# A decoder kernel on one core: half an expert group, a round's values, a batch's weights and two output rows change place

## What is computed

```python
x = x + _L0_attn_ref(_layernorm(x), w_qkv, w_out)          # 16 heads of 8, windows of 64, causal
x = x + _L0_xattn_ref(_layernorm(x), ctx, ctx, times, ...) # 16 heads of 8, keys and values by one of 8 buckets
x = x + _L0_ffn_ref(_layernorm(x), ...)
```

```python
y1 = _ln(x + _mha(x, in_proj_w, ...), ln1_g, ln1_b)   # 4 heads of 32; each group of 8 attends within itself
y2 = _ln(y1 + _moe(y1, wg, w1, b1, w2, b2), ln2_g, ln2_b)

# _moe: 2048 rows, 8 experts, at most 256 rows to each
gates = softmax(xf @ wg); idx = argmax(gates)
keep  = (place of the row within its expert) < 256
h = disp @ w1 + b1                    # no function between the two products
y = h @ w2 + b2
out = where(keep, gate * y, 0)
```

## Time and profile before

| | |
|---|---|
| runs | 343.11, 337.6, 341.99 us; median 341.99 |
| profiled execution | 339.86 us, span 338.1 us |
| TensorE's granted clock, mean | 0.98 |
| busy | PE 317.0 us (94%), DVE 261.2 (77%), ACT 164.7 (49%), POOL 126.8 (38%) |
| transfers | 31.89 MB, mean 94 GB/s |

### The profile page before, as it was taken

The page is one execution under the profiler, slowest core; times in us unless marked ns, Lnnn a source line. Parts: engine busy times, 40 slices in busy tenths (PEclk is TensorE's granted clock), DMA queues, the critical chain, the costliest instruction groups (busy, mean ns, idle before and its releaser), DMA issues.

```text
span 338.1 us, 12320 instructions
## 1 busy us (share of the span) xinstructions
PE 317.0 (94%) x4772; PEld 217.5 (64%) x4772; DVE 261.2 (77%) x663; ACT 164.7 (49%) x454; POOL 126.8 (38%) x208
## 2 busy tenths in 40 slices
PE   7869999999999999999999999989989999998993
PEld 3435556666666565655656556557567769887992
DVE  6874688866666899989899999856456548869996
ACT  2223546666666455463565646554424438633330
POOL 1074556100000345546224344233700006614896
PEclk9976999999999999999999999999999999999998
DMA  4962230636466174589393000000000000125212
GB/s 118 314 180 84 86 121 28 178 116 161 149 154 156 59 183 124 146 196 249 117 214 103 3 2 2 4 5 0 2 2 4 4 0 2 50 80 189 95 33 63
DMA packets 38698, 31.89 MB, mean 94 GB/s; under 512 B 4969, under 2 KB 36209, under 8 KB 38513
## 3 DMA queue, kind: packets, MB, share of 16 engines
q1 hardware_dynamic: 36064, 27.37, 28.9%
q0 software_dynamic: 1280, 3.15, 3.5%
q10 hardware_dynamic: 1296, 0.59, 0.7%
HBM read 23.40 MB, written 7.70 MB: 92 GB/s over the span
## 4 chain that ended last, share of the span: by engine, by line
PE 78%; DVE 10%; issue 5%; POOL 5%; ACT 1%; POOLq 0%; DVEq 0%
PE ps L1262 10%; PE ps L1299 10%; PE ps L1316 10%; PE ps L1272 4%; PE ps L1228 3%; PE ps L1215 3%; PE ps L1236 3%; PE ps L1387 3%; PE ps L1349 3%; PE ps L1332 2%; PE ps L1206 2%; PE ps L1672 2%; PE ps L1405 2%; PE ps L1425 2%; POOL room L909 2%
## 5 line engine op out<-in xcount | busy, mean ns | idle before, releaser
L965 ACT ACTIVATE pT<-ps 128x512 f32<-128x512 f32 x128 | 73.9, 613 | 88.9 <-PE ps L1272 88.9
L833 POOL TENSOR_TENSOR rstd<-veps,minus_half 128x1 f32<-128x1 f32 x32 | 18.8, 588 | 115.5 <-DVE veps L448 115.4
L483 DVE TENSOR_REDUCE m_pad<-ps 128x8 f32<-128x1024 f32 x32 | 39.1, 1221 | 18.1 <-PE ps L1299 17.9
L459 DVE TENSOR_TENSOR p_sb<-qk_sb,heads 128x512 f32<-128x512 f32 x64 | 45.0, 704 | 0.9 <-ACT qk_sb L980 0.5
L486 DVE TENSOR_REDUCE m_pad<-ps 128x8 f32<-128x1024 f32 x32 | 38.9, 1214 | 0.0
L1262 PE MATMUL ps<-p_sb,qk_sb 32*128 32x512 f32 x256 | 38.1, 667 | 0.0
L1299 PE MATMUL ps<-p_sb,qk_sb 32*128 32x512 f32 x256 | 37.7, 659 | 0.0
L1316 PE MATMUL ps<-pT,p_sb 128*32 128x128 f32 x1024 | 35.3, 275 | 0.0
L1672 PE MATMUL ps<-mexp,pT 128*128 128x128 f32 x256 | 31.9, 278 | 1.7 <-DVE pT L777 1.5
L1272 PE MATMUL ps<-mT,negsel 32*128 32x128 f32 x512 | 32.4, 363 | 0.6 <-issue 0.6
L1672 PEld LDWEIGHTS ps<-mexp,pT 128*128 128x128 f32 x256 | 29.8, 192 | 2.5 <-DVE pT L777 2.3
(11 more groups left out here) (197 smaller groups left out, 677.2 us busy)
## 6 DMA issues: line engine op xcount, KB each, us to landing
room<-mask_rows SPq DMA_DIRECT2D x32, 128.0 KB, 3.7
wkv_sb<-wkv SPq DMA_DIRECT2D x23, 128.0 KB
kv_sorted<-room SPq DMA_DIRECT2D x5, 512.0 KB, 3.2
w1t_sb<-w1t SPq DMA_DIRECT2D x8, 256.0 KB
w_sb<-w SPq DMA_DIRECT2D x8, 256.0 KB
kv_sb<-hot_rows SPq DMA_DIRECT2D x4, 512.0 KB, 4.3
ctx_sorted<-room SPq DMA_DIRECT2D x1, 1472.0 KB, 10.0
tk<-fside SPq DMA_DIRECT2D x1, 1024.0 KB
```

The costliest lines, as they stand in the source:

```text
L459: return dve.tensor_tensor(dst, rows.unsqueeze(1).broadcast_to([128, QUADS, S]), heads[:, 0, :].unsqueeze(2).broadcast_to([128, QUADS, S]) ...
L483: dve.tensor_reduce(m4[:, 0:2, 0:QUADS], ps[:, 0:2, :].rearrange("p g (j k) -> p g j k", j=QUADS), AX.X, ALU.max).then_inc(s["max_low"], 1)
L833: pool.tensor_tensor(rstd[:, :], veps[:, :], minus_half[:, :], ALU.pow)\
L965: act.activation(pT[:, t % 2, g, :, :], quad[4 + g], ACT.Exp).then_inc(s["exped"], 1)
```

## The change

Four edits.

1. **Experts.** The first half of group 0 (expert 0) moves from period 31 to the end of period 30, ahead of `y0T_turn`. The second half (expert 1) moves up within period 31, before the output projection, to where the first half was. The other groups stay.
2. **Values of the second round.** TensorE projects them at the end of round 0, ahead of the turned maxima, into bank 0 in place of bank 4, and they wait for the first of the two maxima of round 0. VectorE copies them right after the maxima of round 0. The scores by query of round 1 wait for that copy, since they use bank 0. Rounds 2 and 3 are as before.
3. **Third batch.** The loop over `m` ends three steps earlier. Spreading the picks of batch 2 comes right after `ffn(0)`, and the turning and the logits of the batches 13, 14 and 15 are put around `ffn(1)` and the spreading for batch 3. The turned batches 14 and 15 go to bank 7, columns 256 to 383; `ffn(1)`, in bank 5, waits for the copy of batch 13 where it waited for that of 15.
4. **Rows 12 and 13.** VectorE still subtracts the mean and multiplies by `g2` (L712), now after the statistics of batch 14. ScalarE multiplies by the root, TensorE adds `x + be2` by two products with the identity into bank 0 or 1, and ScalarE copies the sum out. VectorE's two sums for 12 and 13 are gone. Of 14 and 15, both products with `g2` come after the statistics of 15.

The core of the diff:

```diff
@@ in the vector block @@
             def mha_values(i):
                 dve.wait_ge(s["v_done"], i + 1)
-                dve.tensor_tensor(vM[:, 4 * i:4 * i + 4, :], quad[5 if i == 0 else 4],
+                dve.tensor_tensor(vM[:, 4 * i:4 * i + 4, :], quad[(5, 0, 4, 4)[i]],
                                   inb_rows[:, :].unsqueeze(1).broadcast_to([128, QUADS, D]), ALU.add)\
                    .then_inc(s["v_ready"], 1)
...
             for i in range(4):
                 mha_maxima(i)
+                if i == 0:
+                    mha_values(1)
+                if i >= 2:
+                    mha_values(i)
                 if i >= 1:
-                    mha_values(i)
                     mha_outputs(i - 1)
...
                     z_stats(b, 1)
                     if b % 2 and b < B - 2:
                         pair_variance(b, 1)
-                    if b == B - 3:
-                        for a in (b - 1, b):
-                            z_scaled(a, 1, ln_rows[:, 2, :])
                     if b == B - 2:
                         last_variance(b)
-                        z_scaled(b, 1, ln_rows[:, 2, :])
                         for a in (b - 2, b - 1):
-                            z_rows(a, 1, x_sb[:, a, :], y0, "last_rows")
+                            z_scaled(a, 1, ln_rows[:, 2, :])
...
-            z_rows(B - 2, 1, x_sb[:, B - 2, :], y0, "last_rows")
             last_variance(B - 1)
-            z_scaled(B - 1, 1, ln_rows[:, 2, :])
-            z_rows(B - 1, 1, x_sb[:, B - 1, :], y0, "last_rows")
+            for a in (B - 2, B - 1):
+                z_scaled(a, 1, ln_rows[:, 2, :])
+            for a in (B - 2, B - 1):
+                z_rows(a, 1, x_sb[:, a, :], y0, "last_rows")
@@ in the sync block @@
                 if i < B // 2 - 2:
                     sp.wait_ge(s["out_rows"], 2 * i + 2)
                 else:
-                    sp.wait_ge(s["last_rows"], 2)
+                    sp.wait_ge(s["pair_rows"], 2)
@@ in the scalar block, at its end @@
+            for b in (B - 4, B - 3):
+                act.wait_ge(s["rs_ready"], B + B - 1)
+                act.wait_ge(s["w_ready"], B + b - (B - 4) + 1)
+                act.activation(z16[:, b, :], z16[:, b, :], ACT.Identity, scale=rs16[:, b:b + 1])\
+                   .then_inc(s["u_ready"], 1)
+            for b in (B - 4, B - 3):
+                act.wait_ge(s["pair_summed"], b - (B - 4) + 1)
+                act.copy(y0[:, b, :], bank[b % 2][:, 0:D]).then_inc(s["pair_rows"], 1)
             for b in (B - 2, B - 1):
-                act.wait_ge(s["last_rows"], b - (B - 4) + 1)
+                act.wait_ge(s["last_rows"], b - (B - 2) + 1)
                 act.dma_start(out[b:b + 1].rearrange("b s d -> s b d"), y0[:, b:b + 1, :]).then_inc(s["stored"], 16)
@@ in the tensor block @@
-                if p in EXPERT_PERIODS[:2]:
-                    experts(EXPERT_PERIODS.index(p), 0)
+                if p == T - 1:
+                    experts(0, 1)
+                if p == T + 1:
+                    experts(1, 0)
...
-                if p in EXPERT_PERIODS[:2]:
-                    experts(EXPERT_PERIODS.index(p), 1)
-                elif p in EXPERT_PERIODS:
-                    experts(EXPERT_PERIODS.index(p))
+                if p == T - 2:
+                    experts(0, 0)
+                if p == T + 1:
+                    experts(1, 1)
+                if p == T + 3:
+                    experts(2)
...
             def mha_project_v(i):
-                if i >= 1:
+                if i == 1:
+                    pe.wait_ge(s["f_max_low"], 1)
+                if i >= 2:
                     pe.wait_ge(s["f_exped"], 4 * i - 3)
...
                 if i >= 1:
                     pe.wait_ge(s["f_mT_copied"], i)
+                if i == 1:
+                    pe.wait_ge(s["v_ready"], 2)
...
                 mha_by_query(i)
                 if i == 0:
                     mha_by_key(0)
+                    mha_project_v(1)
+                if i >= 2:
+                    mha_project_v(i)
                 if i >= 1:
-                    mha_project_v(i)
                     mha_weighted(i - 1)
...
-            for m in range(B + 7):
+            for m in range(B + 4):
                 project_and_turn(m)
...
-                if m == 19:
-                    place(0)
-                    ffn(0)
-            for b in range(1, B):
-                if b + 1 < QUADS:
-                    spread_hot(b + 1)
+            place(0)
+            ffn(0)
+            spread_hot(2)
+            row_logits(B - 3)
+            turn_row(B - 2)
+            ffn(1)
+            row_logits(B - 2)
+            turn_row(B - 1)
+            spread_hot(3)
+            row_logits(B - 1)
+            for b in range(2, B):
                 ffn(b)
                 if b == 3:
                     turn_picks(1)
                 if b == 4:
                     place(1)
+            for b in (B - 4, B - 3):
+                pe.wait_ge(s["u_ready"], b + 1)
+                pe.matmul(bank[b % 2][:, 0:D], ident[:, :], x_sb[:, b, :], start=True, stop=False)
+                pe.matmul(bank[b % 2][:, 0:D], ident[:, :], z16[:, b, :], start=False, stop=True)\
+                  .then_inc(s["pair_summed"], 1)
```

More of the change, by code:

```diff
@@ L258, in sums_bank, with turned_bank @@
             return 0 if i < 3 else 4
+        def turned_bank(b):
+            return bank[4 + b % 2][:, 0:128] if b < 14 else bank[7][:, 256:384]
         def four_batches(rows, i):
@@ L1109, in turned_row @@
                 act.wait_ge(s["y1T_done"], b + 1)
-                act.activation(y1T[:, b, :], bank[4 + (b % 2 if b < 13 else 1)][:, 0:128], ACT.Identity,
+                act.activation(y1T[:, b, :], turned_bank(b), ACT.Identity,
                                bias=be1_col[:, 0:1]).then_inc(s["y1T_copied"], 1)
@@ L1515, in mha_by_key @@
             def mha_by_key(i):
-                pe.wait_ge(s["v_ready"], i + 1)
+                pe.wait_ge(s["v_ready"], max(i, 1) + (1 if i >= 2 else 0))
                 if i >= 1:
@@ L1593, in _, with turn_row, row_logits @@
             pe.wait_ge(s["aT_ready"], 4)
+            def turn_row(b):
+                if b >= 2:
+                    pe.wait_ge(s["y1T_copied"], b - 1)
+                pe.wait_ge(s["y1_rooted"], b + 1)
+                pe.transpose(turned_bank(b), y1[:, b, :], ident[:, :]).then_inc(s["y1T_done"], 1)
+            def row_logits(b):
+                pe.wait_ge(s["y1T_copied"], b + 1)
+                h, a = divmod(b, B // 2)
+                if b == B // 2:
+                    pe.wait_ge(s["crep_copied"], 1)
+                pe.matmul(bank[6 + h][:, a * E:(a + 1) * E], y1T[:, b, :], wg_sb[:, :], start=True, stop=True)\
+                  .then_inc(s["logits_done"], 1)
             def project_and_turn(m):
@@ L1602, in project_and_turn @@
                       .then_inc(s["f_proj_done"], 1)
[L1603 to L1617 removed]
+                if 0 <= m - 6 < B - 2:
+                    turn_row(m - 6)
+                if 0 <= m - 7 < B - 3:
+                    row_logits(m - 7)
             def turn_picks(h):
@@ L1661, in ffn @@
                 if b < 2:
-                    pe.wait_ge(s["y1T_copied"], 13 if b == 0 else B)
+                    pe.wait_ge(s["y1T_copied"], 13 + b)
                 else:
```

19 lines of the change are left out of this document (2 added, 17 removed).

## The result

| | median us | lowest to highest | runs |
|---|---|---|---|
| before | 339.94 | 336.88 to 343.89 | 22 |
| changed | 337.42 | 334.88 to 339.19 | 22 |

The ratio of changed to before is 0.9938, with a 95% interval of 0.9912 to 0.9965: 2.1 us less, between 1.2 and 3.0. Every ratio in this document leaves out the slow runs, those more than 1.5% above the fastest of their kernel (here five of the kernel before and none of the changed one), while medians and ranges hold all runs; the two medians here lie 2.5 us apart. The forecast was 338.7 us, from 340.9 for the kernel before and a gain of 2.2. The 22 runs put the kernel before at 339.94, and 339.94 - 2.2 = 337.7: of the 1.3 us by which the forecast was too high, 1.0 is the level that it started from.

A forecast was written before the change was run, and what follows sets the result against it. TensorE's chain of waits (78%) with its pauses, and three full queues at the end, were taken as the bound. Gains 0.67 + 0.30 + 1.20 + 0 = 2.17, say 2.2 us, from 340.9 gave 338.7 us; range 335.5 to 341.7.

The forecast's parts named there:

- edit 1: Half group moved into the pause ahead of period 31: period 31 starts 0.12 us later, gain 0.67 us.
- edit 4: Rows 12 and 13 at the end: VectorE loses some 0.6 us, GpSimd nothing; gain 0.
- the two signs of being wrong: VectorE's batch 4 not moved by about 2.2 us; variance of batches 6 and 7 to last power no longer 16.3 us.
- Edit 2: Values of round 1 moved into round 0's pause of 1.06 us: 0.30 of 1.09 us gained, VectorE's reduction being late.
- Stretch B: From the turned maxima of round 0 to the masks of round 1's scores by key; forecast 0.30 us less.
- Edit 3: Among the first expert batches: VectorE starts batch 3 1.26 us earlier and what follows moves too; gain 1.20 us.
- stretch D: From the start of `ffn(0)` to batch 4 on VectorE; forecast 1.20 us less.
- E: Stretch from batch 4 on VectorE to the start of GpSimd's last power; forecast 0 us less.
- the first rival: The end follows VectorE: GpSimd's last rows run freer, edit 4 pays up to 0.7 us, 338.0 us; chance 0.13.
- The router's gain: Rival: the three full queues at the end take back the 1.2 us, giving 339.9 us; chance 0.12.
- held up by 1.06 us: Slower rival: four more GpSimd row calls held behind VectorE's products cost 4.2 us, giving 342.9 us; chance 0.08.
- the pauses closed: Rival: the pauses don't close because what ends them slips too; edits 1 and 2 pay nothing, 339.7 us; chance 0.07.

The follow-up runs named there:

- the one with the pause filled: Kernel before, with four idle bf16 products put behind the scores by key of attention round 0, nothing else moved: 332.55 us, ratio 0.9981.
- the order alone: Changed kernel with the sums of rows 12 and 13 left on VectorE, the rest of VectorE's new order kept: 330.85 us in one run.

## Why the prediction was right, and where it was not

**The sum** holds: 2.30 us in the stretches against 2.17, and 2.1 in the timed runs. It holds partly by luck, since edit 1 gave 0.22 less and edit 4 gave 0.37 more. The first of the two signs of being wrong, a batch 4 on VectorE that has not moved by "about 2.2 us", came out between: it starts 1.93 us earlier against the mark, the missing part being edit 1's. The second did come, and is edit 4's.

**Edit 1: right mechanism, mis-sized term.** What was mis-sized is the handoff, "some 0.04 us at each side (my assumption)". The turned row ends at 225.62 + 0.27 = 225.89 and ScalarE's copy starts at 225.93: 0.04 it is on that side. But the copy ends at 226.20, and TensorE starts period 31 at 226.34, 0.14 us on. So period 31 starts 0.21 later against the mark, not "0.12 later than 224.58", and the exponentials with it. From their end to the weighted sum it is again 0.10 us, not 0.04. That makes 0.14 us of the 0.22 missing. The other 0.07 is a mistake of reading: I took the old start of the weighted sum, 230.10, from the chain of waits, which puts it when the engine was free of the work ahead, and the new one from the timeline's numbers; in the timeline it started at 222.85 + 7.18 = 230.03. With the turn first, the copy is out of the way and the edit gives 0.66.

**Edit 2: right in the profile that I had, and incomplete.** Stretch B went from 5.94 to 5.65, by the two reductions that the prediction named, and the turned maxima follow the second one by 0.15 us. What I didn't ask is what the pause costs besides itself. In the profile before the clock stayed at 1.00 behind it, and so nothing showed. In three of four profiles with the pause unfilled (the kernel before once of twice, edit 2 undone twice of twice) it fell to 0.50 and the stretch took 1.5 to 1.6 us more; in none of the nine that have the values there. On one chip edit 2 undone fell, and edits 1, 3 and 4 undone, with the values in the pause, did not. So the edit is worth 0.3 us in some executions and 1.8 or more in others. How often, these runs leave open: the first timing, 2.1 us by its ratio with an interval of 1.2 to 3.0 and 2.5 by its medians, has room for little beside the 2.3 of the stretches, but its ratio leaves out the longest runs of the kernel before, in which such a fall could lie. The second, 0.9875, is 4.3 us with 2.1 to 6.4, and holds the whole.

**Edit 3: right**, 1.19 for 1.20, mechanism and size. Batch 2 started 1.76 us earlier after `ffn(0)`, with 1.8 forecast, and VectorE paces all from batch 3 on. The new pause of 1.27 us ahead of batch 3, ended by the spreading behind `ffn(1)`, is what is left there. The picks of the second half went out 1.49 us earlier against the mark, 0.75 of it within stretch D, where "no more than those 0.8 us" was forecast; E is as long with the edit as without it, so their transfers held nothing up.

**Edit 4: wrong step.** I wrote "GpSimd loses nothing" and "of the 0.6 us nothing arrives at the end", and my own test for being wrong, the 16.3 us from the variance of batches 6 and 7 to the last power, is now 333.77 - 317.84 = 15.93.

Two readings failed. First, GpSimd's queue was not alone at the end. From "VectorE was done 0.08 us before GpSimd" I took it that the power waited for GpSimd, but 0.08 to 0.09 us is what the handoff from the last variance to the power takes, as the run without the product with g2 shows, where GpSimd stood free. The same 0.08 or 0.09 us stand there in the five other profiles with a late variance: both of the kernel before, the one with the pause filled, edit 4 undone, and the order alone. And GpSimd's last row call ended, at 333.97 + 0.51 = 334.48, 0.04 us ahead of the power, where in the changed kernel the power starts 0.04 us ahead of the shown end of that call (333.36 + 0.45 = 333.81). So the variance ended the wait, and by its own queue GpSimd could have started 0.08 us sooner. The 0.37 us took both: an earlier variance and shorter calls. The variance did get out of the way: it is now 0.79 us ahead of the power, where I said over 0.5.

Second, the calls in that queue are not of fixed length. Even the short ones come in two lengths, 0.45 and 0.51 to 0.53 us, and with VectorE's scalings in the new order they have the shorter one. This is the first rival's direction ("GpSimd's last rows run freer") at half its price, and mostly by another cause than it named: 0.30 of the 0.37 us come with both sums still on VectorE, and there the variance still ends the wait.

In the prediction I cited the Trainium skill, "SBUF — State Buffer", "Who interferes with whom", for a read port that VectorE with two SBUF inputs and GpSimd share. By that rule, too, it is when they meet that counts, and the trace agrees in so far as the order alone changed the calls' lengths; but removing two such sums, for which the rule spoke, was worth 0.07 us. Which pairs of calls meet was not settled: in the kernel with the order alone VectorE's scalings (322.78 to 323.59) lie beside two of GpSimd's calls that take 0.45 us.

The new path of rows 12 and 13 itself was free, as forecast: ScalarE's second copy ends at 333.53, before the last power starts at 333.77.

**The rivals.** The router's gain was not given back: E is 29.84 with edit 3 and 29.83 without. No more of GpSimd's calls were held up by 1.06 us than before. And the pauses closed, the one of edit 1 down to 0.45 us and not to nothing.

## What to carry to other kernels

Measure a small change by stretches between named instructions, from the last one ahead of the change: here they repeat to 0.02 us, the one with the fallen clock apart, where whole runs scatter by 7. Put work that fills a pause behind, not ahead of, the result that another engine waits for: with edit 1 that was 0.21 us beside the 0.45 won. And when a pause of TensorE is priced from one profile, look at the granted clock behind it in a second one: the pause may cost more than its own length.

## What the runs showed of the hardware

- Behind a stand of 1.06 us and another of 0.35, in a stretch where TensorE is otherwise busy, the granted clock fell to 0.50 (1.2 GHz) for some 3 us in three of four profiles. Thirty-two products of the scores went from 1.17 to 1.98 or 2.09 us, and stretch B took 1.5 to 1.6 us more. The nine profiles without the pause of 1.06, none of which shows it, tie it to that pause (the one of 0.35 is there in them too); what decides in which executions it falls is not shown.
- Between profiles the mark alone moves by 9.65 us (214.75 to 224.40), so much of the scatter lies ahead of it. From 20 to 30 us of the span the granted clock was 0.67 in the changed kernel's profile and 0.83 in the timed one of the version with the turn first, whose mark came at 221.00 and not 224.40; in both it is 1.00 from 35 us to 325. These are the two profiles' rows, the second first:

```profile
20.00:30.00 10.00, 8.47 (x93) 4.70 (x96) 5.52 (x10) 3.61 (x11) 6.48 (x7) 0.83 0.50 151
```

```profile
20.00:30.00 10.00, 6.81 (x72) 3.56 (x68) 4.23 (x9) 3.16 (x8) 6.74 (x8) 0.67 0.49 151
```

- The last three of GpSimd's differences on a 128x128 tile (`y<-x_sb,room`) take 0.45 or 0.46 us with VectorE's work in the new order and 0.51 to 0.53 with it in the old one. Six of its row calls in the last 25 us take 1.1 to 1.5 in both.
- From the end of VectorE's last variance to the start of GpSimd's power that waits for it, 0.08 to 0.09 us pass.
